# Order of the first phase: K and V of the first four batches, then of the last four; the context's second rests on GpSimd; four more warming matmuls

## The reference

```python
x = x + tanh(g_xattn) * xattn(layernorm(x), ctx, mask, bias, ln_w, w_q, w_k, w_v, w_out)
x = x + tanh(g_ffn) * ffn(layernorm(x), base_W, gate_W, lora_A, lora_B)
# xattn(h, c): n = rmsnorm(h) * ln_w
#   q, k, v = n @ w_q.T, c @ w_k.T, c @ w_v.T          (4096 columns each: 32 heads)
#   p = masked softmax(q k^T + bias);  return h + (p v) @ w_out.T
```

## Time and profile before

| | us |
|---|---|
| median of three runs | 841.45 (840.96 to 841.49) |
| the profiled execution, its own time | 840.79 |
| span of its trace | 839.0 |
| TensorE busy in the span | 819.3 (98%) |
| VectorE, ScalarE, GpSimd busy | 589.7, 380.1, 429.6 |
| mean granted clock of TensorE | 0.991 of full |

### The profile page before, as it was taken

How to read it: one execution, slowest core, us unless ns; L and a number is a source line. 1 busy time by engine, 2 the same in 40 slices (tenths; PEclk the granted TensorE clock), 3 DMA queues, 4 the chain that set the end, 5 groups by cost and what they waited for, 6 DMA issues and landing times.

```text
span 839.0 us, 14328 instructions
## 1 busy us (share of the span) xinstructions
PE 819.3 (98%) x4270; PEld 703.2 (84%) x4270; DVE 589.7 (70%) x1009; ACT 380.1 (45%) x1042; POOL 429.6 (51%) x402
## 2 busy tenths in 40 slices
PE   8999999999999999879999999999999999998998
PEld 7888888878888899768888888888888888887886
DVE  6985556667635346567788778877887778779852
ACT  5564444456142434364455535553456344642410
POOL 1376656670658265257744675457545764471200
PEclk9999999999999999969999999999999999999999
DMA  8246455453453545855565556555665456644002
GB/s 312 90 147 241 159 178 176 163 174 115 150 195 141 169 174 145 265 205 172 182 237 195 175 176 228 207 182 170 209 225 183 155 206 225 217 144 147 1 26 75
DMA packets 78556, 145.48 MB, mean 173 GB/s; under 512 B 7872, under 2 KB 44736, under 8 KB 76608
## 3 DMA queue, kind: packets, MB, share of 16 engines
q1 hardware_dynamic: 78528, 145.12, 51.3%
HBM read 94.77 MB, written 50.33 MB: 173 GB/s over the span
## 4 chain that ended last, share of the span: by engine, by line
PE 88%; DVE 3%; DMA 3%; issue 2%; ACT 2%; SPq 1%; POOL 1%; DVEq 0%; ACTq 0%; POOLq 0%
PE proj_ps L1836 17%; PE proj_ps L1644 13%; PE proj_ps L1892 12%; PE proj_ps L1911 8%; PE score_ps L1644 7%; PE score_ps L1911 5%; PE proj_ps L1712 4%; PE score_ps L1681 3%; PE proj_ps L2077 3%; PE pv_ps L1911 2%; PE turn_ps L1911 2%; PE turn_ps L1892 2%; PE pv_ps L1892 2%; PE score_ps L1712 2%; PE turn_ps L1681 2%
## 5 line engine op out<-in xcount | busy, mean ns | idle before, releaser
L582 POOL TENSOR_TENSOR comb<-mask_add,bias_sb 128x1024 f32<-128x1024 f32 x32 | 77.3, 2437 | 163.6 <-DVE attn L1406 163.6
L784 ACT ACTIVATE attn<-attn,neg_max 128x128 f32<-128x128 f32 x256 | 99.2, 391 | 35.0 <-DVE neg_max L1395 35.0
L990 ACT ACTIVATE w_hi<-w_raw 128x256 fp32r<-128x256 f32 x105 | 39.8, 413 | 103.1 <-POOL w_raw L656 70.3
L1428 DVE TENSOR_TENSOR acc<-proj_ps,acc 128x512 f32<-128x512 f32 x70 | 48.3, 690 | 37.0 <-PE proj_ps L1644 37.0
L666 POOL TENSOR_TENSOR w_lo<-w_raw,w_hi 128x256 fp32r<-128x256 f32 x105 | 73.3, 738 | 0.0
L1644 PE MATMUL proj_ps<-w_hi,tf_hi 128*128 128x512 f32 x156 | 61.1, 391 | 0.4 <-DVE tf_lo L1424 0.4
L1644 PE MATMUL proj_ps<-w_lo,tf_hi 128*128 128x512 f32 x156 | 60.7, 389 | 0.0
L1644 PE MATMUL proj_ps<-w_hi,tf_lo 128*128 128x512 f32 x156 | 60.7, 389 | 0.0
L618 POOL TENSOR_TENSOR w_lo<-w_raw,w_hi 128x256 fp32r<-128x256 f32 x60 | 46.0, 772 | 24.2 <-ACT w_hi L853 24.1
L1275 DVE TENSOR_TENSOR w_lo<-w_raw,w_hi 128x1024 fp32r<-128x1024 f32 (+1 forms) x21 | 27.9, 1345 | 38.0 <-ACT w_hi L890 38.0
L571 POOL TENSOR_TENSOR w_lo<-w_raw,w_hi 128x1024 fp32r<-128x1024 f32 x20 | 47.7, 2388 | 8.0 <-ACT w_hi L764 8.0
(11 more groups left out here) (334 smaller groups left out, 2530.8 us busy)
## 6 DMA issues: line engine op xcount, KB each, us to landing
w_raw<-in_weights SPq DMA_DIRECT2D x52, 512.0 KB, 5.5
v_sb<-v_spill SPq DMA_DIRECT2D x32, 512.0 KB, 3.7
q_spill<-attn SPq DMA_DIRECT2D x60, 256.0 KB, 3.0
qt<-q_spill SPq DMA_DIRECT2D x15, 1024.0 KB, 4.8
block_spill<-block_sb SPq DMA_DIRECT2D x30, 512.0 KB, 3.5
attn<-block_spill SPq DMA_DIRECT2D x120, 128.0 KB, 2.9
w_raw<-in_v_weights SPq DMA_DIRECT2D x12, 512.0 KB, 4.2
v_spill<-v_sb SPq DMA_DIRECT2D x12, 512.0 KB, 4.8
```

What stands on the lines that cost most here:

```text
L582: pool.tensor_tensor(comb[:, j, :, :], mask_add[:, :, :], bias_sb[:, j:j + 1, :].to_broadcast([P, B, S]), ALU.add).then_inc(comb_done, 1)
L784: e = act.activation(probs[:, u, i, :], probs[:, u, i, :], ACT.Exp, bias=neg_max[:, u, i:i + 1], accum_out=row_sum[:, u, i:i + 1])
L1428: dve.tensor_tensor(acc[:, b, :], out_banks[b][:, :], acc[:, b, :], ALU.add).then_inc(acc_done, 1)
```

## The change

K is computed for the first four batches, then V for these four, then K for the last four (in the same two banks as the first) and V of batches 4 and 5; V's products of the first four batches use banks 2 and 3. V's weights, x0 and x1 are loaded in front of the context's second half. ScalarE's list follows that. The four rests of the context's second half move from VectorE to GpSimd, one in front of the first inverse root and three behind it, with a semaphore of their own (`ctx_lo2_done`). On VectorE the rest of V's weights moves up, and the second half's variances move behind the norms of tiles 2 and 3. TensorE gets two warming matmuls behind the rounding of K's first weight half and two behind the rounding of the first context chunk.

```diff
@@ -269,7 +269,7 @@
 
         w_hi_done = [sem(f"w_hi_done{k}") for k in range(4)]
         w_lo_done = [sem(f"w_lo_done{k}") for k in range(4)]
-        ctx_hi_done, ctx_lo_done = sem("ctx_hi_done"), sem("ctx_lo_done")
+        ctx_hi_done, ctx_lo_done, ctx_lo2_done = sem("ctx_hi_done"), sem("ctx_lo_done"), sem("ctx_lo2_done")
         ident_zero, ident_done, pow_const, ids_done = sem("ident_zero"), sem("ident_done"), sem("pow_const"), sem("ids_done")
 
         dve_step = sem("dve_step")
@@ -328,11 +328,11 @@
             sp.dma_start(w_raw[:, WK, WN // 2:WN], weights[0, WK][:, WN // 2:WN]).then_inc(w_in[WK], 16)
             load_ctx(2, 0)
             load_ctx(3, 0)
+            load_w(WV, 0)
+            load_x(0)
+            load_x(1)
             for c in range(C):
                 load_ctx(c, 1)
-            load_x(0)
-            load_x(1)
-            load_w(WV, 0)
             load_x(2)
             load_x(3)
             sp.dma_start(lnw[:, :], ln_w.rearrange("(a n) -> a n", a=1).to_broadcast([P, D])).then_inc(small_in, 16)
@@ -592,8 +592,16 @@
             pool.tensor_tensor(w_lo[:, WV, 0:WN // 2], w_raw[:, WV, 0:WN // 2], w_hi[:, WV, 0:WN // 2].bitcast(F32),
                                ALU.subtract).then_inc(wv_half_lo, 1)
             pool.wait_ge(pow_const, 1)
-            for g in range(2):
-                inverse_root(g + 1, slice(g * G, (g + 1) * G), 2)
+            def rest_ctx(c):
+                pool.wait_ge(ctx_hi_done, C + c + 1)
+                pool.tensor_tensor(ct_lo[:, c, half(1)], ctx_raw[c][:, half(1)], ct_hi[:, c, half(1)].bitcast(F32),
+                                   ALU.subtract).then_inc(ctx_lo2_done, 1)
+
+            rest_ctx(0)
+            inverse_root(1, slice(0, G), 2)
+            for c in range(1, C):
+                rest_ctx(c)
+            inverse_root(2, slice(G, B), 2)
             rest(WQ, 0)
 
             def s_forms(i):
@@ -817,17 +825,17 @@
             act.activation(w_hi[:, WK, WN // 2:WN], w_raw[:, WK, WN // 2:WN], ACT.Copy).then_inc(w_hi_done[WK], 1)
             lead_ctx(2, 0)
             lead_ctx(3, 0)
+            act.wait_ge(w_in[WV], 16)
+            act.activation(w_hi[:, WV, 0:WN // 2], w_raw[:, WV, 0:WN // 2], ACT.Copy).then_inc(wv_half_hi, 1)
+            act.activation(w_hi[:, WV, WN // 2:WN], w_raw[:, WV, WN // 2:WN], ACT.Copy).then_inc(w_hi_done[WV], 1)
+            for m in range(2):
+                copy_proj(0, m, m, k_at(m))
             for c in range(C):
                 lead_ctx(c, 1)
             for m in range(2):
-                copy_proj(0, m, m, k_at(m))
-            act.wait_ge(w_in[WV], 16)
-            act.activation(w_hi[:, WV, 0:WN // 2], w_raw[:, WV, 0:WN // 2], ACT.Copy).then_inc(wv_half_hi, 1)
-            act.activation(w_hi[:, WV, WN // 2:WN], w_raw[:, WV, WN // 2:WN], ACT.Copy).then_inc(w_hi_done[WV], 1)
-            for m in range(2, UNITS):
-                copy_proj(0, m, m, k_at(m))
+                copy_proj(0, 2 + m, 2 + m, v_dst(m))
             for m in range(2):
-                copy_proj(0, UNITS + m, m, v_dst(m))
+                copy_proj(0, UNITS + m, m, k_at(2 + m))
             act.wait_ge(small_in, 48)
             act.activation(tanh_g[:, :], gates[:, :], ACT.Tanh).then_inc(tanh_done, 1)
             lead(WQ, 0)
@@ -1146,7 +1154,7 @@
                 return dve.tensor_scalar(root_of[:, 0, at], mean_var[:, at, 1], EPS, None, ALU.add)
 
             def rest_ctx(c, t):
-                dve.wait_ge(ctx_hi_done, t * C + c + 1)
+                dve.wait_ge(ctx_hi_done, c + 1)
                 dve.tensor_tensor(ct_lo[:, c, half(t)], ctx_raw[c][:, half(t)], ct_hi[:, c, half(t)].bitcast(F32),
                                   ALU.subtract).then_inc(ctx_lo_done, 1)
 
@@ -1161,8 +1169,7 @@
             rest_w(WK, slice(WN // 2, WN), w_hi_done[WK], w_lo_done[WK])
             rest_ctx(2, 0)
             rest_ctx(3, 0)
-            for c in range(C):
-                rest_ctx(c, 1)
+            rest_w(WV, slice(WN // 2, WN), w_hi_done[WV], w_lo_done[WV])
 
             def rest_xt(i, hi_done, lo_done, banks):
                 dve.wait_ge(hi_done, i + 1)
@@ -1209,14 +1216,13 @@
             x_stats(0)
             ordered(x_stats(1))
             x_variances(0)
-            rest_w(WV, slice(WN // 2, WN), w_hi_done[WV], w_lo_done[WV])
             x_stats(2)
             refine(1, first, 2)
             dve.wait_ge(small_in, 48)
             norm_x(0, range(G // 2))
             ordered(x_stats(3))
+            norm_x(0, range(G // 2, G))
             x_variances(1)
-            norm_x(0, range(G // 2, G))
             for i in range(G):
                 rest_xt(i, xt_hi_done, xt_lo_done, xn_ps)
             refine(2, second, 2)
@@ -1762,19 +1768,20 @@
                         pe.wait_ge(wk_half_lo, 1)
                     if t == 0 and c == 2:
                         pe.wait_ge(w_lo_done[WK], 1)
-                    pe.wait_ge(ctx_lo_done, t * C + c + 1)
+                    pe.wait_ge((ctx_lo_done, ctx_lo2_done)[t], c + 1)
                 return wait
 
 
             pe.wait_ge(ident_done, 1)
             for _ in range(WARM):
                 pe.matmul(score_ps[0][:, 0:P], ident[:, :], ident[:, :], start=True, stop=True)
-            for t in range(2):
+            def first_keys(t):
+
                 wait = k_pieces(t)
                 for c in range(C):
                     wait(c)
                     for j in range(HP):
-                        o = proj_ps[t * HP + j][:, :]
+                        o = proj_ps[j][:, :]
                         at = slice(c * HP * DH + j * DH, c * HP * DH + (j + 1) * DH)
                         for n, (l, r) in enumerate(((0, 0), (1, 0), (0, 1))):
                             mm = pe.matmul(o, w2[l][:, WK, at], ct2[r][:, c, half(t)], start=(c == 0 and n == 0), stop=(c == C - 1 and n == 2))
@@ -1786,15 +1793,25 @@
                 if c == 2:
                     pe.wait_ge(w_lo_done[WV], 1)
 
-            for m in range(3):
-
-                pe.wait_ge(proj_copied, m + 1)
-                v_one(2 * m, m, v_halves if m == 0 else None)
-                if m == 2:
-                    turn_xn(0)
-                    turn_xn(1)
-                v_one(2 * m + 1, m).then_inc(proj_done, 1)
+            pe.wait_ge(wk_half_hi, 1)
+            for _ in range(2):
+                pe.matmul(score_ps[0][:, 0:P], ident[:, :], ident[:, :], start=True, stop=True)
+            pe.wait_ge(ctx_hi_done, 1)
+            for _ in range(2):
+                pe.matmul(score_ps[0][:, 0:P], ident[:, :], ident[:, :], start=True, stop=True)
+            first_keys(0)
+            for m in range(2):
+                v_one(2 * m, 2 + m, v_halves if m == 0 else None)
+                v_one(2 * m + 1, 2 + m).then_inc(proj_done, 1)
+
+            pe.wait_ge(proj_copied, 2)
+            first_keys(1)
+            turn_xn(0)
+            turn_xn(1)
+            pe.wait_ge(proj_copied, 3)
+            v_one(4, 2)
             turn_xn(2)
+            v_one(5, 2).then_inc(proj_done, 1)
             turn_xn(3)
 
             pe.wait_ge(proj_copied, UNITS)
```

## The result

The changed kernel takes 844.42 us in the median of seven executions (843.75 to 846.5), the kernel before 841.45 beside it (seven, 840.96 to 842.4). The ratio is 1.0039, its 95% interval 1.0029 to 1.0049: **slower by 0.39%, 3.3 us**. The forecast was +6.1 us. The profiled execution took 844.42, its span is 842.4 (before 839.0), so the traces differ by 3.4.

What follows compares the result with a forecast made beforehand. TensorE, busy 819.3 of 839.0 us, bounds the kernel. Warming 0, Q's delay 4.6 and the clock drop 1.5 sum to +6.1, taking the median from 841.45 to 847.6 us; range from 842.5 less its error up to 850.2.

Steps and rivals of the forecast that it cites:

- The three Newton steps: VectorE, from 19.4: each step waits for one GpSimd rest of 1.29 us plus about 0.1; norms start at 23.5.
- From the first norm to `var_done`: VectorE: two pairs of norms with statistics between, then variances, 7.45 us, from 23.5 to 30.95.
- V follows K without a wait: TensorE: K's first half ends at 12.53, V is ready at 12.5, the wait at 19.12 goes.
- the warming: TensorE before 6.96: four more matmuls are worth 0, between -0.1 and +0.2 us.
- The clock: TensorE behind the 3.3 us stop at Q: about 3 us at half rate, costing 1.5 us.
- case A: The forecast itself: VectorE and GpSimd exclude each other and the clock drops, 847.6 us; chance 0.45.
- The loads: Start of kernel: V's weights land at about 10.5, x0 at 11.9, x1 at 13.2, the last gate at 19.8.
- The first root: GpSimd's first inverse root runs from 17.5 to 19.4, instead of 18.63 to 20.58.
- Q's rest and TensorE's start behind it: GpSimd rounds Q's weight rest in 2.57 us, to 35.5; TensorE starts Q 0.24 later, at 35.75.
- the wait at K: TensorE in K of the second half: starts at 18.3, waits 1.0 us at 19.7, ends at 24.8.
- the 4.6: TensorE's start of Q: 4.6 us late, at 35.75 instead of 31.15, losses at K and the turns included.
- Rival C: No exclusion, or the small steps slip in between: Q at 32.2, +1.05, 842.5 us; chance 0.16.

Runs made afterwards that it cites:

- b_warm: The kernel before with only the four added warming matmuls: 841.03 us, ratio 1.0001.
- a_var_first: The changed kernel with the second half's variances back in front of the norms of tiles 2 and 3: 843.51 us, ratio 1.0033.
- a_rests_on_dve: The changed kernel with the four rests of the context's second half back on VectorE: 844.55 us, ratio 1.0033.
- reorder_alone: The changed kernel with the four context rests back on VectorE and the variances first again, keeping new order, loads and warming: 840.76 us, ratio 1.0002.
- best1: The changed kernel with three context rests on VectorE, one on GpSimd, variances first, third turn behind V of batch 5: 839.18 us, ratio 0.9987.
- a_fill: The changed kernel with nine identity matmuls on TensorE in front of Q's wait: 842.04 us, ratio 1.0011.
- a_gap: The changed kernel with GpSimd's last three context rests held until VectorE's first norm is done: 843.30 us, ratio 1.0036.

## Why the prediction was right in sign and too large

**Right.** Slower, inside the range, by the mechanism and at the instruction named: Q waits for GpSimd's rest `w_lo` L571, behind the second root, behind `var_done`. The three Newton steps each wait for one rest (1.24, 1.21, 1.22). From the first norm to `var_done` 7.45 us were forecast, and 7.44 measured. V follows K without a wait; the warming is worth nothing (b_warm). The clock falls behind the stop and costs 1.6 us where 1.5 was taken, so case A was the one that happened. In this there was luck: the prediction took a drop because a stop of 3.3 us is nearer to 3.56, which dropped the clock, than to 1.7, which did not. The stop was 2.29, nearer to 1.7, and a_var_first's of 2.36 dropped nothing. By its own argument the prediction would have left out the 1.5.

**Mis-sized.** Q was put at 35.75 and came at 33.31. The 2.44 us in which the sum was too high are, in its own terms:

- *The loads, 1.11.* V's weights were ready for ScalarE at 9.62 and not 10.5, and the statistics of x ran from 12.09, right behind V's rest, not from 13.1. VectorE's `var_done` came at 16.24 instead of 17.35. The step that failed is the reckoning from one landing rate of the kernel before. b_warm's trace shows 1.3 us of difference between two executions for the same load, which is the error this term should have had.
- *The first root, 0.29, and the second, 0.28.* They were taken at 1.95 and 1.87 from the earlier trace rows. Both had been held up there by VectorE's two-input work; free they take 1.65 and 1.64. The sentence that the root takes no part in the exclusion, since it had not slowed L1204, looked only at one of the two sides.
- *The Newton steps, 0.32.* The three took 3.78 us with their gaps, not 4.1: just the time of GpSimd's three rests (17.94 to 21.72), which follow one another at about 1.26 and not 1.29 + 0.1.
- *Q's rest and TensorE's start behind it, 0.43.* 2.35 instead of 2.57, again taken from a row in which L1204 ran until 28.65, and 0.05 instead of 0.24. The 0.24 was read as TensorE's start behind Q's rest, while by the ends of the rows TensorE was waiting for the fourth rest of the turned x, until 31.04.

**Wrong: the wait at K.** One of 1.0 us was forecast at 19.7. There was none, since the rests, some 1.5 us earlier than forecast (the second ended at 19.23, not 20.7), kept ahead of TensorE. It was inside the 4.6, so it costs nothing in the sum; but TensorE was at Q at 31.0 and not at 32.5, and its stop was 2.29 and not 3.3.

**A row misread.** The prediction takes L1146 at 16.75 (1.12 us) as two-input work. Its code adds a constant to one tensor in SBUF, and still it ended with GpSimd's L592 (17.86, 17.84). The other two rows it names are of two-input instructions. The sum doesn't hang on it, since the Newton steps have two inputs, but "two SBUF inputs" is then not the whole condition.

**Incomplete: the weight of the two parts.** The prediction presented GpSimd's rests as the cost. Against the kernel before they make 0.57 of the 2.80 by which `var_done` is later; 2.23 are the pair of norms put in front of the variances, a term that stood in the chain to Q and that none of the rivals priced by itself. That is the sum along one chain, though, and doesn't say what either part is worth. The four kernels with the new order do:

| ratio | variances behind the norms | variances first |
|---|---|---|
| rests on GpSimd | 1.0039 (changed) | 1.0033 (a_var_first) |
| rests on VectorE | 1.0033 (a_rests_on_dve) | 1.0002 (reorder_alone) |

Either part alone costs about what both cost together, 0.3% (the three intervals overlap). Taking the blocking away gains 0.42 us at Q in one trace (a_rests_on_dve), since the last gate is the next thing to hold the norms: at 19.8 by the earlier trace rows, with norms from 20.0 to 21.4 in the traces where it held them. Taking the norms' new place away gains 0.45 at Q, since the turn is next (a_var_first). Only both together bring the time back, and only best1, which also moves the turn, wins anything. Rival C, "no exclusion, +1.05", has its nearest run in a_rests_on_dve, at 1.0033: there the norms started at 21.37 and not at 20.0, VectorE had the rests to do, and the half clock came all the same.

**After Q.** The prediction saw nothing that gives the delay back, and that holds up to the middle: 3.74 us at 42.72, and 4.2 at 357.59 (the same matmul starts at 361.77). The end is 3.4 later. Between 345 and 373 us the wait of 3.56 for `attn` and that of 3.22 for `tf_lo` come back, as 4.9 and 3.6, but with two short half-clock stretches instead of the long one of the earlier trace rows:

```profile
358.00:361.00 3.00, 0.00 (x0) 1.00 0.82 211
361.00:366.00 5.00, 3.61 (x16) 0.66 0.63 215
366.00:369.00 3.00, 0.07 (x1) 0.97 0.85 287
369.00:373.00 4.00, 4.00 (x11) 0.60 0.45 184
```

Before, the clock stood at half for 13.6 us here, as it did in a_rests_on_dve; in the changed kernel and in a_fill it was 6.8, in best1 10.2. In the table +2.46 at 40 us became +0.5 at the end in a_fill, and +3.30 became +4.4 in a_rests_on_dve. Matmul for matmul they were 2.8 and 3.75 late at 340 us, so most of both changes came in this stretch. What decides how it falls was not settled. It is why the medians, not one span, carry the verdicts here.

## What to carry to other kernels

When two neighbours in an instruction list change places, price the one that now comes later, and then what is next late at each step: here three nearly equal limits (gates, turns, Q's rest) stood behind one another, and taking one away moved Q by 0.45 us at most, and the time came back only when both parts were undone. Undoing one part of a change and seeing no gain doesn't show that the part is free. GpSimd work beside VectorE work with two SBUF inputs is worst beside a chain of tiny dependent instructions, each of which waits for a whole one of the other engine; put it beside VectorE's statistics (L1186 took its usual 0.67 to 0.69 us each beside L597) or where VectorE reads PSUM, as L1176 does beside Q's rest. A stop that can't be removed may be filled with matmuls: behind nine of them the clock stayed up, and the trace is 1.6 us shorter from Q to the next wait.

## What the runs showed of the hardware

- The root on GpSimd (L588, 128 x 8) takes 1.64 to 1.65 us beside statistics, beside L1176 or alone, 1.87 beside the norms, and 1.95 to 2.04 beside the rests on VectorE. It was itself never seen to stretch a VectorE instruction.
- Stops of TensorE of 2.29, 2.29 and 2.19 us (changed kernel, a_rests_on_dve; a_gap's at K) were followed by half a clock within some 1.1 us, one of 2.36 (a_var_first) was not, nor those of 1.69 and 1.72 (reorder_alone). The length of the stop alone does not decide it.
- The last gate's load, issued in the same place, let the norms start at 20.03, 20.13 and 21.37 us in three traces.
- The same 18 warming records took 3.74 us before and 4.21 in the changed kernel; K started at 6.96 and 7.05.
- Beside Q's rest a Newton step of the second half took 1.75 us in the changed kernel (L1146 at 31.53), 0.16 in the kernel before, where Q's rest was over; the two-input L1176, one of whose inputs lies in PSUM, kept its 0.68 beside it.
